# Expert feed-forward one token tile at a time instead of two tiles per pass over the weights

## What is computed

```python
x = x + attn(layernorm(x))                      # ends in: combined @ Wout
# feed-forward on h = layernorm(x), one row per token
probs = softmax(h @ gate_w.T)                   # 8 experts
combine = one_hot(top2(probs)) * weight / sum   # zero for six of the eight
eo = (silu(h @ w_gate[e]) * (h @ w_up[e])) @ w_down[e]     # for every e; 1024 -> 1408 -> 1024
out = sum_e combine[:, e] * eo + sigmoid(h @ shared_gate) * shared_expert(h)
x = x + out
```

## Time and profile before

| | us |
|---|---|
| timed runs, median of 2 | 6111.06 (5931.71 and 6290.40) |
| profiled execution, its own time | 5880.41 |
| its span, slowest core (core 7) | 5878.9 |
| spans of the eight cores | 5855.1 to 5878.9 |

### The profile page before, as it was taken

One profiled execution on the slowest core, in us unless ns is written; L12 is line 12 of the kernel. 1 busy time (PEld: TensorE's weight loads), 2 busy tenths in 40 slices (PEclk: granted clock), 3 DMA queues, 4 the chain that ended last, 5 costly groups with the idle time before them and its releaser, 6 DMA issues.

```text
span 5878.9 us, 65354 instructions; the slowest of 8 cores (5855.1 to 5878.9 us)
## 1 busy us (share of the span) xinstructions
PE 5003.7 (85%) x24644; PEld 2333.1 (40%) x24644; DVE 1440.2 (24%) x3633; ACT 1430.8 (24%) x3547; POOL 133.2 (2%) x225
## 2 busy tenths in 40 slices
PE   3555555569999999799999997999999979999999
PEld 1333333324444444344444443444444434444444
DVE  1445444431111111311111113111111131111111
ACT  1334334331212112312121213211212132121121
POOL 0000000000000000000000000000000000000000
PEclk9666666679999999899999998999999989999999
DMA  8777777421122111311211122122111311221112
GB/s 172 179 183 181 176 179 182 127 114 60 60 99 79 60 60 76 114 60 59 112 66 60 59 95 96 59 78 100 60 60 60 113 42 60 99 79 59 59 62 86
DMA packets 85699, 555.83 MB, mean 95 GB/s; under 512 B 7824, under 2 KB 7824, under 8 KB 63632
## 3 DMA queue, kind: packets, MB, share of 16 engines
q0 software_dynamic: 60496, 475.56, 26.3%
q1 hardware_dynamic: 24896, 76.09, 3.7%
HBM read 526.48 MB, written 103.02 MB: 107 GB/s over the span
## 4 chain that ended last, share of the span: by engine, by line
PE 74%; ACT 2%; DVE 2%; issue 1%; DMA 1%; DVEq 0%; ACTq 0%; SPq 0%
PE psf L1076 25%; PE psf L1018 23%; PE psf L1022 23%; PE psf L828 2%; ACT silu_sb L1034 1%; ACT ucp_sb L1035 1%; DMA x_sb<-x 1%; DVE h_sb L1044 1%; PE psb L751 0%; ACT h_sb L155 0%; DVE xln2T L761 0%; DVE combT L761 0%; DVE xln2T L765 0%; ACT el_sb L918 0%; DVE cmask L934 0%
## 5 line engine op out<-in xcount | busy, mean ns | idle before, releaser
L1076 PE MATMUL psf<-wring,h_sb 128*128 128x512 bf16 x6336 | 1460.0, 394 | 153.8 <-DVE h_sb L1044 153.8
L1034 ACT ACTIVATE silu_sb<-psf 128x512 bf16<-128x512 f32 x792 | 472.9, 597 | 3389.2 <-PE psf L1022 3389.2
L1076 PEld LDWEIGHTS psf<-wring,h_sb 128*128 128x128 bf16 x6336 | 635.0, 101 | 978.8 <-issue 295.9
L1044 DVE TENSOR_TENSOR h_sb<-silu_sb,ucp_sb 128x512 bf16<-128x512 bf16 x792 | 337.0, 426 | 2440.5 <-ACT ucp_sb L1035 2440.5
L1018 PE MATMUL psf<-combT,wring 128*128 128x512 bf16 x3168 | 755.1, 381 | 0.6 <-ACT ucp_sb L1035 0.3
L1022 PE MATMUL psf<-combT,wring 128*128 128x512 bf16 x3168 | 750.9, 380 | 0.0
L1018 PE MATMUL psf<-xln2T,wring 128*128 128x512 bf16 x3168 | 748.4, 379 | 0.0
L1022 PE MATMUL psf<-xln2T,wring 128*128 128x512 bf16 x3168 | 748.4, 379 | 0.0
L1092 DVE SCALAR_TENSOR_TENSOR x_sb<-psf,c_sb,x_sb 128x512 f32<-128x512 f32 x576 | 432.8, 751 | 1115.9 <-PE psf L1076 1115.9
L1018 PEld LDWEIGHTS psf<-combT,wring 128*128 128x128 bf16 x3168 | 310.6, 98 | 378.4 <-issue 9.7
L1022 PEld LDWEIGHTS psf<-combT,wring 128*128 128x128 bf16 x3168 | 310.8, 98 | 376.9 <-issue 5.6
(11 more groups left out here) (113 smaller groups left out, 2193.9 us busy)
## 6 DMA issues: line engine op xcount, KB each, us to landing
wring<-wbf POOLq DMA_DIRECT2D x108, 2816.0 KB, 11.7
wbf<-stg POOLq DMA_DIRECT2D x36, 1408.0 KB, 5.5
x_sb<-x SPq DMA_DIRECT2D x64, 512.0 KB, 7.8
stg<-wg POOLq DMA_DIRECT2D x16, 1408.0 KB, 11.5
stg<-wu POOLq DMA_DIRECT2D x16, 1408.0 KB, 11.2
out<-x_sb SPq DMA_DIRECT2D x32, 512.0 KB, 4.7
wbf<-stg POOLq DMA_DIRECT2D x9, 1536.0 KB, 6.1
stg<-wd POOLq DMA_DIRECT2D x8, 1536.0 KB, 12.4
```

Source lines behind the costliest of these rows:

```text
L1034: sc.activation(silu_sb[:, (it % 2) * SC:(it % 2 + 1) * SC], gb, AF.Silu)
L1044: ins = v.tensor_mul(h_sb[:, hb + it * SC:hb + (it + 1) * SC], silu_sb[:, (it % 2) * SC:(it % 2 + 1) * SC], ucp_sb[:, (it % 2) * SC:(it % ...
L1076: ins = t.matmul(db, h_sb[:, hb + it * SC + tloc * C:hb + it * SC + (tloc + 1) * C], wring[:, wd0 + it * D + dc * 512:wd0 + it * D + (dc + ...
```

## The change

The pair disappears. Phase 2 now loops over the 8 tiles, and each tile runs its whole prelude (a and then b) and then all nine experts. Every expert's three matrices are therefore loaded again for every tile: `NPIECES` goes from 108 to 216. A piece's slot is free as soon as the one tile is done with it. The ring, the order of the pieces, the matmuls, the activations and the router's arithmetic stay as they are.

Around that:

- `combT` and `xln2T` each have one use again, and `xln2_bf` holds the normalised tile; nothing is borrowed from `h_sb`. The waits that kept the borrowed buffers and the router's PSUM columns of two tiles apart are gone.
- The first load brings `comb` and `x` of tile 0 only: 8 DMAs in place of 12, `comb` and `x` in turn.
- `x` of tile t + 1 is loaded during tile t, behind the load of `comb` for t + 1; it waits only for tile t - 1's residual add. It was loaded for two tiles at once, once in a pair.
- A tile's store is queued behind its own experts. `c8_sb` and `el_raw` shrink to one tile.

```diff
-NPIECES = PPT * (NTILE // 2)
+NPIECES = PPT * NTILE
...
-        for pair in range(NTILE // 2):
-            t0, t1 = 2 * pair, 2 * pair + 1
...
-            emit_pre_a(t0, combT, xln2_bf)
-            emit_pre_a(t1, xln2T, h0)
-            wlast = wout_done_hist[t1]
-            emit_pre_b(t0, combT, xln2_bf, wlast)
-            emit_pre_b(t1, xln2T, h0, wlast)
...
+        for t_i in range(NTILE):
...
+            if t_i == 0:
+                S("sld").n += 128
+                def ld0(s, tgt=S("sld").n, xcur=xcur):
+                    for tt in range(4):
+                        s.dma_start(out=combt_sb[:, tt * D:(tt + 1) * D],
+                                    in_=comb_h[tt * C:(tt + 1) * C, :]).then_inc(S("sld").h, 16)
+                        ins = s.dma_start(out=xcur[:, tt * D:(tt + 1) * D],
+                                          in_=x_h[tt * C:(tt + 1) * C, :])
+                        ins.then_inc(S("sld").h, 16)
+                    s.wait_ge(S("sld").h, tgt)
...
+            emit_t512b(combt_sb, combT, s12[:, 0:8], s12[:, 8:16])
...
+            if t_i + 1 < NTILE:
+                S("sld").n += 64
+                def ldx2(s, t_n=t_i + 1, wtgt=wout_done_hist.get(t_i - 1, 0), tgt=S("sld").n):
+                    if wtgt:
+                        s.wait_ge(S("vcw").h, wtgt)
...
+            ln2_done = emit_ln_sc(x1, xln2_bf, per_tt_wait=vcw_tloc)
+            em("tensor", lambda t, tgt=ln2_done: t.wait_ge(S("sc1").h, tgt))
+            emit_t512b(xln2_bf, xln2T)
...
             for e in range(NEXP):
-                p0 = PPT * pair + 3 * e
-                for tp in range(2):
-                    t_i = t0 + tp
+                p0 = PPT * t_i + 3 * e
+                hb = (e % 2) * NIT * SC
...
-                    if tp == 1:
-                        piece_done[p0] = ("scg", S("scg").n)
-                        piece_done[p0 + 1] = ("scg", S("scg").n)
+                piece_done[p0] = ("scg", S("scg").n)
+                piece_done[p0 + 1] = ("scg", S("scg").n)
...
-                    if tp == 1:
-                        piece_done[p0 + 2] = ("ped", S("ped").n)
+                piece_done[p0 + 2] = ("ped", S("ped").n)
```

More of the change, by code:

```diff
@@ L836, in vwout @@
                     def vwout(v, tloc=tloc, dc=dc, bk=bk, tgt=S("pew").n, x1=x1, xcur=xcur,
-                              sttgt=(store_tgts.get(t_i - 2) if gidx == 0 else None)):
+                              sttgt=(store_tgts[t_i - 2] if (gidx == 0 and t_i >= 2) else None)):
                         v.wait_ge(S("pew").h, tgt)
@@ L849, in emit_pre_a @@
             wout_done_hist[t_i] = wout_done
[L851 to L855, removed]
-                    for tp in range(2):
[L857 to L861, removed]
+            if t_i + 1 < NTILE:
[3 more added lines that the diff above has]
+                        s.wait_ge(S("vcw").h, wtgt)
+                    for tt in range(4):
+                        ins = s.dma_start(out=x_sb[:, ((t_n) % 2) * 4 * D + tt * D:((t_n) % 2) * 4 * D + (tt + 1) * D],
+                                          in_=x_h[t_n * SC + tt * C:t_n * SC + (tt + 1) * C, :])
+                        ins.then_inc(S("sld").h, 16)
                     s.wait_ge(S("sld").h, tgt)
                 em("sync", ldx2)
[L864 to L870, removed]
+            ln2_done = emit_ln_sc(x1, xln2_bf, per_tt_wait=vcw_tloc)
+            em("tensor", lambda t, tgt=ln2_done: t.wait_ge(S("sc1").h, tgt))
+            emit_t512b(xln2_bf, xln2T)
             xln2T_done = S("vct").n
-            c0 = c8off[t_i]
-            c0r = c0
             rreg = [(0, 0), (1, 0), (0, 16), (1, 16)]
@@ L895, in emit_trt @@
                 em("tensor", trt)
-            emit_trt(0, wait_cp=router_cp_tgts.get(t_i - 1))
+            emit_trt(0)
             emit_trt(1)
@@ new lines, in build_nc, with st @@
+            tile_done = S("vcd").n
+            ssem = "sstA" if t_i % 2 == 0 else "sstB"
+            S(ssem).n += 64
+            store_tgts.append((ssem, S(ssem).n))
+            def st(s, t_i=t_i, tgt=tile_done, ssem=ssem,
+                   fin=(S("sstA").n, S("sstB").n), x1=x1):
+                s.wait_ge(S("vcd").h, tgt)
+                for tt in range(4):
+                    ins = s.dma_start(out=out_h[t_i * SC + tt * C:t_i * SC + (tt + 1) * C, :],
+                                      in_=x1[:, tt * D:(tt + 1) * D])
+                    ins.then_inc(S(ssem).h, 16)
+                if t_i == NTILE - 1:
+                    s.wait_ge(S("sstA").h, fin[0])
+                    s.wait_ge(S("sstB").h, fin[1])
@@ L1127, in build_nc @@
+            em("sync", st)
         em.flush_block()
```

274 lines of the change are left out of this document (106 added, 168 removed).

## The result

| | before | after |
|---|---|---|
| timed runs, median | 5951.8 us (12 runs, from 5881.4) | 6056.3 us (13 runs, from 5941.1) |
| ratio of the compared runs | | 1.0089, 95% interval 1.0049 to 1.0129 |
| profiled execution, its own time | 5880.4 us | 5946.9 us |
| spans of the eight cores | 5855.1 to 5878.9 us | 5914.8 to 5945.4 us |

The change makes the kernel about 0.9% slower. A good part of the executions of either kernel run with one die at a lower granted clock and take up to 14% longer; the medians contain them, and the ratio leaves them out.

A forecast was written before the change was run, and what follows sets the result against it. TensorE was taken to bound the kernel. Core 4: 5872.1 + 71 (preludes, first units) - 5 (first load) + 11 (weight waits) = 5949, 5951 with 1.5 us between span and time, moved to 5965; range 5890 to 6130.

The forecast's parts named there:

- The bound and the preludes: Phase 2: TensorE bounds the kernel; single-tile preludes and the slower first units behind them add 71 us in all.
- The lost overlap: Preludes of a pair: two single ones take 92.7 us against 77.61 overlapped, 15.1 us more for each pair.
- The first unit's 42.76 us: Gate and up behind a prelude take 42.76 us where later units take 40.10; once more per pair, 2.66 us.
- The weight loads: Expert changes in phase 2: the 108 more loads stay hidden and cost nothing on a core like core 7.
- The cover: Expert change: time left between the gate and up load landing and the next gate matmul, read as 0 to 2 us.
- The first load: Before the first prelude: four fewer DMAs, 2.1 MB, shorten TensorE's wait for x by 5 us, at most 16.
- The contention term: Expert changes on disturbed cores: each core's weight waits double, 11.2 us more on core 4; bounds nothing and 179 us.
- The number: Whole kernel: forecast time 5965 us, put between the summed 5951 and 6003, nearer the profiled execution.
- Within 2%, the same: Outcome class for the whole kernel: a change within 2%, about what a measurement can tell from no change, chance 0.79.
- The weights as the bound: Rival at expert changes: each unit's start waits for gate and up weights; 5998 to 6125 us, chance 0.16.
- The shift of the clock: Rival in the down projections: new preludes shift which take 19.15 or 20.84 us; 5870 to 5992 us, chance 0.08.
- A hidden cost in the prelude: Rival in the preludes: a single tile's chain meets a wait the pair hid; 5998 to 6050 us, chance 0.05.

The follow-up runs named there:

- kernel with hidden preludes: The changed kernel with the prelude of tile t+1 sliced between blocks of tile t's experts, all 216 loads kept: ratio 0.9742 to the kernel before, profiled 5761.6 us.
- store runs: The changed kernel with an extra store to DRAM queued ahead of gate loads: profiled 6134.4 us with 2.1 MB, 5986.1 us with 1.05 MB.
- first-load run: The changed kernel with x of tile 1 in the first load again: TensorE's first wait for x 43.9 us in the mean, against 38.9 in the changed kernel.
- serial pair: The kernel before with its 108 loads, but in each pair tile 0's whole prelude comes before tile 1's: ratio 1.0147 to the kernel before.

## Why the prediction was right or wrong

**The bound and the preludes: right.** The lost overlap was the term of 15.1 us per pair. A single prelude was put at 46.3 us; the eight on core 7 take 43.5 to 46.7, 45.8 in the mean. The first unit's 42.76 us came back eight times, at 42.8 to 43.1. The working from tile 0's rows held because those stretches were undisturbed by tile 1 in the kernel before. Core 7 went from 4715.1 us between its first weight load and the end (5878.9 - 1163.8) to 4781.9 (5935.5 - 1153.6): 66.8 us, where 66 had been summed. Over the eight cores it is 59.7 to 78.1 us, 66.5 in the mean; the 78.1 are core 4's, for which the sum with its waits was 77. Row by row on core 7, the eight preludes take 366.2 us where the four of pairs took 310.1, 56 more (60 forecast), and the first units behind them are 12 us longer in all (11 forecast).

**Beside the rows,** the Trainium skill (TensorE: Matmul & The Clock Gate, "The HAM clock gate (the "warmup" mystery)") says that TensorE's clock halves in idle time and returns with work. The trace agrees at the prelude shown (13.76 us idle, then 3.57 us for eight matmuls that take 1.89 at full clock). In the kernel with hidden preludes a pause of 2.3 us was followed by a fall too, at 53 of 72 down projections on core 6.

**The weight loads: right.** Apart from waits on single cores, which come below, they stay hidden, as the run with twice the loads in pairs and the one with half of them tile by tile show. The cover was read as 0 to 2 us; the store runs and the landings give about 2.6.

**The first load: right,** 5.0 us over the eight cores; on core 7 alone the wait fell by 3.0 us, from 40.6 to 37.6.

**The contention term: right in size for core 4, wrong in its rule.** I doubled each core's waits. Core 4 had 11.2 us and now has

```profile
PE psf L975 <- DMA wring<-wbf: 20.6, 18, 2.8
```

but core 3, with 14.5 us before, now has

```profile
PE psf L975 <- DMA wring<-wbf: 3.0, 3, 1.3
```

where 29 was expected. Over the eight cores the waits went from 26.8 to 23.9 us. They were 25.2 with twice the loads in pairs and 12.0 with half the loads tile by tile, but also 12.3 in the first-load run with all 216 loads, and cores 4 to 7 of the serial pair wait 18.9 us with its 108 loads, where they had 11.2 before. They don't follow the number of expert changes. I had put them down to how far apart two neighbours run, and had read 5 to 8 us between cores 4 and 5 from the earlier trace rows. That reading doesn't hold: the times of each core count from that core's own first instruction, so they don't say when two cores loaded at the same time. What decides the waits stays open.

**The number: wrong, at the last step of the sum.** The sum gave 5951 us for an execution like the profiled one, and such an execution took 5946.9, 1.1% over 5880.4. The sum was 1.2% more; the compared runs give 0.9%, with an interval that holds 1.2% and excludes zero. But two things were done to that sum. It was moved to 5965, between 5951 and the 6003 that the same ratio gives on the lower of the two timed runs; and it was left beside a median of 6111 us for the kernel before, under which 5965 reads as a gain of 2.4%. The mechanism said slower and the number said faster. The two timed runs were 6% apart, so neither their median nor a point between them was a base to add 70 us to. With more runs the median of the kernel before is 5951.8 us, 159 us below the one shown, while its profiled execution, 5880.4, and its lowest run, 5881.4, are 1 us apart. The forecast should have been the ratio, 1.012, carried to whatever base is used.

**"Within 2%, the same": too coarse.** The chances treated a change of 1.2% as no change. The whole interval of the ratio lies above 1, and the five compared runs of the changed kernel lie within 6.3 us of each other. A sum of 66 to 71 us whose terms each come from rows was a forecast of slower, by a small amount, and should have been said so.

**The rivals.** The weights as the bound did not happen; by the store runs their threshold of 0.8 us per change lies between 1.05 MB more at each change (0.36 us) and 2.1 MB more (2.4 us). The shift of the clock did not happen either: 22 of the 72 down projections on core 7 are short ones in the kernel after, the rest long, where it was 24 before. A hidden cost in the prelude did not exist in the changed kernel, but did in the serial pair, where the router's tail came bare.

## What to carry to other kernels

When loops are reordered for one resource (weight traffic, buffers), price what the old order overlapped: here 108 more loads of 2.9 MB cost no time that could be measured, and eight preludes without a partner, with the slower first units behind them, cost 68 us. A stage that makes the busiest engine wait for the others is better cut into slices and laid between that engine's blocks than paired with its like; that gave 185 us where pairing gave 68. A pause of 2.3 us ahead of a long block cost another 1.69 us through the clock in about three of four cases (53 of 72 on core 6), and both go away if the block starts with the operands that are ready.

## What the runs showed of the hardware that I had not expected

A pause of 2.3 us on TensorE was followed by a lower granted clock at most down projections: 53 of 72 on core 6 took 1.69 us longer, and over the first 6 us of the one shown it was 0.72, a mixture of 1.2 and 2.4 GHz. With the pause gone the clock stays at 1.00 over 4200 us of dense matmuls, on all eight cores at once.

Cores of the chip wait for weights by amounts that vary from core to core and run to run (0 to 20.6 us per core without the stores) and do not grow with the number of loads, but grow sharply with the length of each: 24, 186 and 1204 us over the eight cores with 0, 1.05 and 2.1 MB ahead of each change.
